# Receptance token mix on GpSimd in the layer-1 time mixing: one kernel, one core

## The reference

```python
shifted = jnp.concatenate([jnp.zeros_like(x[:, :1, :]), x[:, :-1, :]], axis=1)
xk = x * time_mix_k + shifted * (1.0 - time_mix_k)
xv = x * time_mix_v + shifted * (1.0 - time_mix_v)
xr = x * time_mix_r + shifted * (1.0 - time_mix_r)
k = jnp.einsum('bsd,ed->bse', xk, Wk)
v = jnp.einsum('bsd,ed->bse', xv, Wv)
r = jax.nn.sigmoid(jnp.einsum('bsd,ed->bse', xr, Wr))
wkv = _wkv(k, v, time_decay, time_first)      # a scan over the 256 tokens
out = jnp.einsum('bsd,ed->bse', r * wkv, Wo)
```

## Time and profile before

| | before |
|---|---|
| median of 3 runs | 3756.96 us (3754.93 to 3757.32) |
| profiled execution, its time | 3792.08 us |
| profiled execution, its span | 3790.4 us |
| PE / DVE / ACT / POOL busy in the span | 76% / 60% / 40% / 18% |
| first turning matmul of the stage to its last addition | 2087.9 to 2512.2 us |

### The profile page before, as it was taken

One profiled execution on the slowest core, in us unless ns is written; L12 is line 12 of the kernel. 1 busy time (PEld: TensorE's weight loads), 2 busy tenths in 40 slices (PEclk: granted clock), 3 DMA queues, 4 the chain that ended last, 5 costly groups with the idle time before them and its releaser, 6 DMA issues. The chain is left out here.

```text
span 3790.4 us, 61007 instructions
## 1 busy us (share of the span) xinstructions
PE 2869.0 (76%) x21640; PEld 2226.4 (59%) x21641; DVE 2280.1 (60%) x3963; ACT 1510.4 (40%) x2470; POOL 669.8 (18%) x640
## 2 busy tenths in 40 slices
PE   4999877777650079999800999969999999367797
PEld 3666655555550068888700888846666666246686
DVE  5544567777541111111154788869999999788642
ACT  1232344434210012222100666648888888268100
POOL 0111012233206600000165000011111110000500
PEclk9999988888655589999955999979999999789898
DMA  3000241111012254444332000000000000024444
GB/s 106 0 0 0 82 149 53 51 52 52 17 38 97 87 182 143 142 141 142 112 92 89 1 1 1 1 22 15 13 13 13 15 13 10 24 122 188 173 149 165
DMA packets 112116, 261.90 MB, mean 69 GB/s; under 512 B 15168, under 2 KB 55104, under 8 KB 103232
## 3 DMA queue, kind: packets, MB, share of 16 engines
q1 hardware_dynamic: 93888, 206.95, 15.8%
q0 software_dynamic: 18048, 52.45, 4.2%
HBM read 169.17 MB, written 90.18 MB: 68 GB/s over the span
## 5 line engine op out<-in xcount | busy, mean ns | idle before, releaser
L1797 DVE TENSOR_SCALAR e_low<-bank 128x2048 f32<-128x2048 f32 x128 | 293.1, 2290 | 37.6 <-PE bank L1669 34.5
L1190 ACT ACTIVATE cx_h<-bank,cx_b 128x256 f32<-128x256 f32 x288 | 120.7, 470 | 406.4 <-PE bank L1144 406.4
L1144 PE MATMUL bank<-cx_zT,cx_w 128*128 128x256 f32 x1152 | 262.2, 381 | 1.8 <-DVE cx_zT L1199 1.8
L1155 PE MATMUL bank<-cx_w,cx_h 128*128 x1152 | 260.4, 379 | 0.0
L1621 ACT ACTIVATE e_low<-e_low 128x2048 f32<-128x2048 f32 x128 | 245.1, 1915 | 2.1
L1618 ACT ACTIVATE e_low<-e_low 128x2048 f32<-128x2048 f32 x128 | 243.5, 1903 | 0.0
L1144 PEld LDWEIGHTS bank<-cx_zT,cx_w 128*128 128x128 f32 x1152 | 219.9, 191 | 32.5 <-DMA cx_w<-cw_dram 1.3
L2163 PE MATMUL bank<-f_wout,fd_q 128*128 128x256 f32 x1024 | 223.2, 381 | 19.5 <-DVE fd_q L2182 19.5
L1155 PEld LDWEIGHTS bank<-cx_w,cx_h 128*128 128x128 f32 x1152 | 213.4, 190 | 26.1
L1798 DVE TENSOR_SCALAR e_high<-bank 128x1536 f32<-128x1536 f32 x128 | 223.8, 1748 | 0.0
L2163 PEld LDWEIGHTS bank<-f_wout,fd_q 128*128 128x128 f32 x1024 | 195.9, 191 | 46.8 <-DVE fd_q L2182 19.8
(11 more groups left out here) (353 smaller groups left out, 6833.7 us busy)
## 6 DMA issues: line engine op xcount, KB each, us to landing
cx_w<-cw_dram SPq DMA_DIRECT2D x72, 512.0 KB
hidden<-fu_h SPq DMA_DIRECT2D x32, 1024.0 KB, 3.9
fd_h<-hidden SPq DMA_DIRECT2D x32, 1024.0 KB, 4.8
cx_rows<-slot_rows SPq DMA_DIRECT2D x72, 256.0 KB, 3.6
slot_y<-cx_y POOLq DMA_DIRECT2D x72, 256.0 KB
X<-x_dram SPq DMA_DIRECT2D x4, 2048.0 KB, 11.8
g_cT<-ctxT_dram SPq DMA_DIRECT2D x32, 256.0 KB, 5.3
queries<-g_qT SPq DMA_DIRECT2D x32, 256.0 KB, 6.2
```

What stands on the lines that cost most here:

```text
L1144: last = nc.tensor.matmul(H[k][f // 2][:, (f % 2) * GROUP_ROWS:(f % 2 + 1) * GROUP_ROWS], w1[k][:, c, f * P:(f + 1) * P], zT[k][:, c, :], ...
L1155: last = nc.tensor.matmul(Y[k][:, n * D:(n + 1) * D], h[k][:, f, n * P:(n + 1) * P], w2[:, bass.ds(e, 1), f, :].rearrange("p o d -> p (o d ...
L1190: nc.scalar.activation(h[k][:, f, :], H[k][f // 2][:, (f % 2) * GROUP_ROWS:(f % 2 + 1) * GROUP_ROWS], ACT.Gelu, bias=b1[:, bass.ds(e, 1), ...
L1797: nc.vector.tensor_scalar(flat(low[n % RING][:]), HEADS4.rearrange("p r s -> p (r s)"), -1.0, 0.0, ALU.mult, ALU.max).then_inc(neg_ready, 1)
```

## The change

GpSimd makes the receptance's mixed input itself, as (z - z_before) * time_mix_r + z_before, in three tensor_tensor instructions for each batch on the turned tile: `step`, `part_r`, `mix_r` (two buffers). TensorE's `receptance` takes `mix_r` with the plain weights `w[2]`, four matmuls where there were eight, and waits for `mix_ready`. `now` and `before` lose their third members, and so DVE four of its twelve weight scalings.

```diff
@@ layer1_rwkv: tiles
-        now = [sb(f"now{m}", [P, DC, D]) for m in "kvr"]
-        before = [sb(f"before{m}", [P, DC, D]) for m in "kvr"]
+        now = [sb(f"now{m}", [P, DC, D]) for m in "kv"]
+        before = [sb(f"before{m}", [P, DC, D]) for m in "kv"]
+        step, part_r = sb("step", [P, DC, S]), sb("part_r", [P, DC, S])
+        mix_r = [sb(f"mix_r{k}", [P, DC, S]) for k in TWO]
...
-        INIT, CONSTS, WEIGHTS = 6, 6 + DC, 6 * DC
+        INIT, CONSTS, WEIGHTS = 6, 6 + DC, 4 * DC
@@ gpsimd, behind the memsets
+            pool.wait_ge(w_in, 80)
+            pool.wait_ge(setup, INIT)
+            for b in range(B):
+                pool.wait_ge(zT_ready, b + 1)
+                at, last = zT[b % 2][:, :, 1:S + 1], zT[b % 2][:, :, 0:S]
+                if b:
+                    pool.wait_ge(part_ready, b)
+                nc.gpsimd.tensor_tensor(step[:], at, last, ALU.subtract).then_inc(step_ready, 1)
+                pool.wait_ge(step_ready, b + 1)
+                if b:
+                    pool.wait_ge(mix_ready, b)
+                nc.gpsimd.tensor_tensor(part_r[:], step[:], cols[:, 2, :, None].to_broadcast([P, DC, S]), ALU.mult).then_inc(part_ready, 1)
+                pool.wait_ge(part_ready, b + 1)
+                if b > 1:
+                    pool.wait_ge(r_raw, b - 1)
+                nc.gpsimd.tensor_tensor(mix_r[b % 2][:], part_r[:], last, ALU.add).then_inc(mix_ready, 1)
@@ tensor: receptance(b)
-                project(b, 2, R[b % 3], r_raw)
+                pe.wait_ge(mix_ready, b + 1)
+                for e in range(DC):
+                    for c in range(DC):
+                        last = nc.tensor.matmul(R[b % 3][:, e * S:(e + 1) * S], w[2][:, c, e * P:(e + 1) * P], mix_r[b % 2][:, c, :], start=c == 0, stop=c == DC - 1)
+                last.then_inc(r_raw, 1)
@@ vector: weight scalings (L1517 and L1522)
-            for m in range(3):
+            for m in TWO:
```

More of the change, by code:

```diff
@@ L1294, in layer1_rwkv @@
         names = ("w_in", "setup", "wexp", "consts", "weights", "shift", "z", "zT_raw", "zT", "k_raw", "v_raw", "r_raw", "pp", "h", "arg", "ex", "abs", "er",
-                 "ev", "state", "prod", "nd", "whole", "ln", "gate_in", "gate", "y", "o_raw", "x_done")
+                 "ev", "state", "prod", "nd", "whole", "ln", "gate_in", "gate", "y", "o_raw", "x_done", "step", "part_r", "mix_r")
         (w_in, setup, wexp, consts, weights, shift_ready, z_ready, zT_raw, zT_ready, k_raw, v_raw, r_raw, pp_ready, h_ready, arg_ready, ex_ready, abs_ready, er_ready,
-         ev_ready, state_ready, prod_ready, nd_ready, whole_ready, ln_ready, gate_in, gate_ready, y_ready, o_raw, x_done) = (sem(n) for n in names)
+         ev_ready, state_ready, prod_ready, nd_ready, whole_ready, ln_ready, gate_in, gate_ready, y_ready, o_raw, x_done, step_ready, part_ready, mix_ready) = (sem(n) for n in names)
         K, V, R, T = bank[0:2], bank[2:4], bank[4:7], bank[7]
```

## The result

| | before | after |
|---|---|---|
| median | 3757.06 us (4 runs, 3754.93 to 3757.32) | 3793.11 us (4 runs, 3790.23 to 3794.69) |
| ratio | | 1.0096, 95% interval 1.0079 to 1.0114 |
| profiled execution, time / span | 3792.08 / 3790.4 us | 3793.34 / 3791.7 us |
| first turning matmul of the stage to its last addition | 2087.9 to 2510.7 us | 2053.3 to 2514.5 us |

The account below looks back on a forecast made before the run. PE looked like the bound at 12.53 us a batch, over an ACT-DVE loop of 11.86; blocking adds 2.45, giving 14.31. Terms 52.3 + 1.4 - 1.7 = +52 us on 3756.96 give 3809 us, range 3797 to 3822.

Parts of the forecast that it names:

- The bound: Stage loop: PE looks like the bound at 12.53 us a batch; ACT and DVE's own loop sets a floor of 11.86 us.
- TensorE's saving: Receptance matmuls: eight passes fewer, about 1.7 us a batch, of which only 0.67 us can reach the period.
- The blocking and its turns: L1471 to L1495 beside `step`, `part_r`, `mix_r`: POOL and two-SBUF-input DVE instructions alternate, waiting engine next; 2.45 us a batch.
- The rival without blocking: L1471 to L1495: POOL and DVE don't block each other; period 11.86 us, 3736 us in all; chance 0.07.
- the one in which VectorE goes on: L1471 to L1495: DVE continues with issued instructions, POOL enters at the next PSUM instruction; 12.46 us, about 3753 us; chance 0.08.
- part of the turns: L1471 to L1495: one blocked instruction less, 1.0 to 1.2 us less a batch, 3770 to 3795 us; chance 0.15.
- the recursion: From L1470's start s: end times of alternating POOL and DVE instructions, 0.13 us off for overlap, until L1495 ends at s+6.53.
- all the turns: L1471 to L1495: the full sequence of turns, period 14.31 us, 3809 us, range 3797 to 3822 us; chance 0.62.
- The sum: Whole stage: +52.3 us for 29 periods, +1.4 for L1470(0) to L1470(1), -1.7 for the first batch; together +52 us.
- The clock: TensorE's clock falls as PE pauses: at 0.83 nothing happens, half speed throughout 220 us more; clock or other extra cost 0.06.
- the sign that I named for it: Granted clock of the stage under 1.00 would show the rival in which TensorE's clock falls.
- Two signs: Steady window: PE busy for about 76%; and the wait of ACT's L1341 for PE's receptance matmuls vanishes.

Follow-up runs that it names:

- experiment 2: Changed kernel without GpSimd's mix, TensorE multiplying the unshifted zT with plain weights in four matmuls; 3738.01 us, ratio 0.9951 to the kernel before.
- experiment 3: Changed kernel with GpSimd's mix of batch b begun only when `whole` of batch b-2 is written; 3736.67 us, ratio 0.9946 to the kernel before.
- experiment 5: Changed kernel with two write-only memsets in place of each GpSimd tensor_tensor, TensorE multiplying zeros; 3738.66 us, ratio 0.9953 to the kernel before.
- experiment 8: Late start of experiment 3, but receptance from zT with eight matmuls and the mix thrown away; 3757.03 us, ratio 0.9996 to the kernel before.
- experiment 1: Changed kernel, GpSimd's mix made and waited for but thrown away, receptance from zT with eight matmuls; 3796.23 us, ratio 1.0106 to the kernel before.
- experiment 4: Changed kernel with the start of GpSimd's mix tied to the end of maxima, where ratio begins; 3779.20 us, ratio 1.0060 to the kernel before.
- Experiment 7: Kernel of experiment 3 plus sixteen GpSimd additions of 128x512 in eight input forms behind the last batch; 3759.12 us in a single run.

## Why the prediction was right, and where it was off

**The bound** was read right. The loop of ScalarE and VectorE at 11.86 us, seen in one early batch, is what experiments 2, 3 and 5 run at, to 0.01 us.

**TensorE's saving**, at most 0.67 us a batch: confirmed by experiments 3 and 8, some 20 us.

**The blocking and its turns** were right in kind, order and place. Experiment 5 shows that it takes a read on GpSimd's side. That of these VectorE instructions only those with two SBUF inputs take part is shown by `step`, which keeps its 1.04 us beside a running L1492, and by experiment 3, where L1494 begins beside a running `mix_r` and keeps its 1.22 us; L1492's own 1222 ns in the changed kernel would prove nothing, as it was there first. The rival without blocking falls with experiment 1, the one in which VectorE goes on and "part of the turns" with the timeline of after. The turns are shown only as far as this: whoever had waited goes next. GpSimd's three instructions each wait for the semaphore of the one before and so start 0.08 us behind its end; whether VectorE would get its turn between GpSimd instructions issued back to back, no run here tried. The step from the rule of the Trainium skill ("SBUF — State Buffer", section "Who interferes with whom") to "turns" had no support in the page; the runs give it.

**The size** was off, mostly in one term, GpSimd's own time. I took 1.27 us for `step` and `mix_r` from L584; they take 1.04 and 1.18 us (and `part_r` 1.04 for 1.05). Redone with these and nothing else changed, the recursion's last end falls by 0.33 us, and the delay from 2.45 to about 2.1 us. The trace has 2.02. The rest is in the overlap, for which I took 0.13 us throughout: VectorE's blocked instructions end their own time less 0.11 to 0.14 us behind GpSimd's, but GpSimd's two end their own time less 0.20 and 0.21 us behind VectorE's. Experiment 7 says why L584 was the wrong row: it multiplies two different tiles, whereas `step` reads one tile twice. The second stage's L580, the square of one tile, has that form and 1.04 us, and its row lies in the prediction's own evidence. I read it there for where it stood, and not for its shape.

The right mechanism with too large a size has a consequence for the chances. 3793 us lies outside the 3797 to 3822 us that I gave to all the turns, and inside the 3770 to 3795 us that I gave to "part of the turns" (0.15). By the time alone one would have picked the wrong case; the stretched instructions and experiments 1, 3 and 4 decide it.

**The sum**, by its parts, in the profiled executions. First turning matmul to L1470(0): 19.5 in place of 21.7 us, -2.2 (I had -1.7, the eight matmul passes; the other 0.5 us is that TensorE's clock rises earlier in the first `keys`: the first group of four passes takes 1.92 us in both kernels, where it is 1.03 us later on, but the third group takes 1.28 us in the changed kernel and 1.76 us in that of before). To L1470(1): 12.34 in place of 11.26, +1.1 (I had +1.4, with the longer turns). The 29 periods from there: 2085.16 to 2487.99, 402.8 us, against 2120.82 to 2483.32, 362.5: +40.3 (I had +52.3; 29 times the 0.43 us by which the delay was too large is 12.5). The last period: 11.85 in place of 12.09, -0.2 (I had 0). Together +39.0 us. What comes behind the last L1470 took 0.6 us less, which makes the 38.4 of the whole stage; between the medians it is 36.

**The clock** was no cost. In the steady part TensorE now pauses for L1517, for at most 2.2 us a batch, and its granted clock in the window is 0.98; in stretches of 50 us between 2150 and 2450 us it goes down to 0.93. In experiment 1, with eight matmuls, it is 1.00 in the same window and the period is the same 13.89 us, so the lower clock costs the changed kernel nothing. I had given "at most about 3 us" of pause and little chance to a cost from a fall, which was right; the sign that I named for it (under 1.00) shows all the same, and so was a poor sign.

**Two signs did not come.** TensorE's busy share is 83%, not the 76% that I expected. At the measured period my 10.8 us of work would be 78%; for the rest, I divided the distances of its matmuls by the period, while the profile's busy time counts their longer durations (argued, not worked out further). And ScalarE's wait for the receptance matmuls has not vanished: 67.2 us in 28 times, where it was 120.4. It costs nothing, since ScalarE then has to wait for VectorE's maxima anyway.

## What to carry to other kernels

Before work is moved to an idle GpSimd, list VectorE's instructions around the place by where their inputs lie: beside those with an input in PSUM GpSimd's reads were free here, and so they were beside the batch_norm statistics, which read one tensor. One input is no licence in general: the tensor_scalar L2180 and L2182 of the earlier trace rows read one tensor each and take turns with GpSimd all the same (1.28 to 2.28 us, and 1.23 to 2.17). Beside VectorE instructions with two SBUF inputs, a GpSimd instruction that had to be waited for in full cost VectorE 0.72 to 0.93 us, for 1.04 to 1.18 us of its own. One wait on the right semaphore moved the same three instructions from a loss of 36 us to a gain of 20 us. And when the busiest engine is relieved, look for a batch in the trace in which it isn't late: its period is the floor that the relief can reach.

## What the runs showed of the hardware

That a float32 scan and a scalar_tensor_tensor with two SBUF inputs stand in the same queue as a tensor_tensor (1222 to 1515 ns in the changed kernel; 692 to 1411 ns in experiment 4) I had expected only for the first. New to me was the price of a GpSimd tensor_tensor of 128x512 float32: 1.04 us when both inputs are of one tile or one is a spread column, 1.18 to 1.27 us with two tiles.
